# A graph network in float32: a deeper ring in its degree pass, a later `result`, and loads moved between queues

## The reference

```
h   = relu(layernorm(x))
A   = relu((adj + adj.T) / 2);  D = rowsum(A);  s = D ** -0.5
x   = x + relu((I - s[:,None] * A * s[None,:]) @ (h @ W0))        # layer 0
h   = relu(layernorm(x))
x   = x + diag(adj) @ h @ W1[0] + triu(adj,1) @ h @ W1[1] + tril(adj,-1) @ h @ W1[2] + bias   # layer 1
```

## Time and profile before

| what | value |
|---|---|
| median of 3 runs | 955.57 us (954.47 to 959.18) |
| profiled execution | 955.61 us |
| its span | 953.9 us |
| PE busy | 912.2 us, 96% |
| DVE, ACT, POOL busy | 554.6, 487.0, 289.6 us |
| moved by DMA | 212.69 MB, mean 223 GB/s |
| granted clock of PE, mean | 0.995 |

### The profile page before, as it was taken

One profiled execution on the slowest core, in us unless ns is written; L12 is line 12 of the kernel. 1 busy time (PEld: TensorE's weight loads), 2 busy tenths in 40 slices (PEclk: granted clock), 3 DMA queues, 4 the chain that ended last, 5 costly groups with the idle time before them and its releaser, 6 DMA issues.

```text
span 953.9 us, 17244 instructions
## 1 busy us (share of the span) xinstructions
PE 912.2 (96%) x4471; PEld 768.4 (81%) x4471; DVE 554.6 (58%) x1475; ACT 487.0 (51%) x1026; POOL 289.6 (30%) x300
## 2 busy tenths in 40 slices
PE   3679999999999999999999999899999999999998
PEld 2558778888888888888888888688888888888886
DVE  4899677778787766565656565333333443344432
ACT  3797567676766765545554554233333333333331
POOL 4895344434434444443344332011111100000000
PEclk9999999999999999999999999899999999999999
DMA  9995899999999985556555653766666655555552
GB/s 285 328 282 146 282 326 328 341 325 346 336 328 335 323 316 179 159 178 196 164 158 176 195 192 113 237 185 191 190 182 188 190 167 164 168 162 159 163 169 68
DMA packets 179578, 212.69 MB, mean 223 GB/s; under 512 B 13648, under 2 KB 114000, under 8 KB 177488
## 3 DMA queue, kind: packets, MB, share of 16 engines
q1 hardware_dynamic: 136816, 158.18, 54.4%
q10 hardware_dynamic: 42720, 54.01, 15.9%
HBM read 143.99 MB, written 68.16 MB: 222 GB/s over the span
## 4 chain that ended last, share of the span: by engine, by line
PE 84%; DVE 4%; DMA 4%; issue 3%; POOL 2%; SPq 2%; ACT 1%; ACTq 0%; DVEq 0%; POOLq 0%
PE psAcc L579 23%; PE psAcc L577 23%; PE psAcc L578 23%; PE psG L548 2%; PE psG L550 2%; PE psA L453 2%; PE psG L549 2%; PE psZ L489 2%; DMA colb<-in_adj 2%; DMA xp<-in_x 2%; PE psW L425 1%; POOL AT L1099 1%; PE psAcc L591 1%; PE psAcc L589 1%; PE psAcc L590 1%
## 5 line engine op out<-in xcount | busy, mean ns | idle before, releaser
L645 ACT ACTIVATE Lh<-C 128x512 fp32r<-128x512 f32 x256 | 161.3, 630 | 300.5 <-PE psAcc L579 250.1
L577 PE MATMUL psAcc<-Xh,Lh 128*128 128x512 f32 x496 | 200.2, 404 | 4.1 <-DVE Ll L838 4.0
L577 PE MATMUL psAcc<-Yh,Lh 128*128 128x512 f32 x512 | 200.9, 392 | 0.0
L579 PE MATMUL psAcc<-Yh,Ll 128*128 128x512 f32 x512 | 200.1, 391 | 0.0
L578 PE MATMUL psAcc<-Yl,Lh 128*128 128x512 f32 x512 | 199.9, 390 | 0.0
L579 PE MATMUL psAcc<-Xh,Ll 128*128 128x512 f32 x496 | 195.0, 393 | 0.0
L578 PE MATMUL psAcc<-Xl,Lh 128*128 128x512 f32 x496 | 194.4, 392 | 0.0
L838 DVE TENSOR_TENSOR Ll<-C,Lh 128x512 fp32r<-128x512 f32 x128 | 90.8, 711 | 148.8 <-ACT Lh L645 148.8
L579 PEld LDWEIGHTS psAcc<-Yh,Ll 128*128 128x128 f32 x512 | 96.1, 188 | 20.3
L578 PEld LDWEIGHTS psAcc<-Yl,Lh 128*128 128x128 f32 x512 | 96.2, 188 | 19.0
L577 PEld LDWEIGHTS psAcc<-Xh,Lh 128*128 128x128 f32 x496 | 93.8, 189 | 21.6 <-issue 4.9
(11 more groups left out here) (134 smaller groups left out, 1348.0 us busy)
## 6 DMA issues: line engine op xcount, KB each, us to landing
C<-at_dram SPq DMA_DIRECT2D x128, 256.0 KB, 2.7
at_dram<-AT SPq DMA_DIRECT2D x16, 1088.0 KB, 5.4
s_dram<-C ACTq DMA_DIRECT2D x64, 256.0 KB, 5.3
R<-in_adj SPq DMA_DIRECT2D x64, 256.0 KB, 5.8
g_dram<-g ACTq DMA_DIRECT2D x32, 512.0 KB, 3.3
C<-s_dram SPq DMA_DIRECT2D x64, 256.0 KB, 3.9
C<-in_adj SPq DMA_DIRECT2D x60, 256.0 KB, 5.3
t_dram<-x ACTq DMA_DIRECT2D x32, 256.0 KB, 2.2
```

The costliest lines, as they stand in the source:

```text
L577: mm(acc, lh, rh[:, k, :], start=k == 0, stop=False)
L579: mm(acc, ll, rh[:, k, :], start=False, stop=c < L1 and k == NB - 1).then_inc(used, 1)
L645: A(Lh[:, q, :], C[:, q, :], ACT.Relu if s.c < L1 else ACT.Copy).then_inc(lhi, 1)
```

## The change

It does five things. The ring `sring` holds six chunks instead of four, so that DVE's sum n waits for ACT's and POOL's work on chunk n-6; there are four sets of statistics instead of three; yTs becomes a seventh turn buffer. The loads of the weights and of the first two tiles of x go from SP's queue to the head of ACT's, and PE waits for the weights only before the first product with W0. `load_next` no longer loads R for step 2: SP issues these four loads at the end of the prologue, each after PE's transposes of step 1's R. The load of the next xp is split off `turned_xp` as `load_xp`, and in step 1 it is called earlier in ACT's body. `result` of step 34 moves to where that of step 33 is: ahead of `split_lo(nxt, 2)`.

```diff
+RING = 6
...
-            sring = sb("sring", [P, 4, 4 * P], at=early)
+            sring = sb("sring", [P, RING, 4 * P], at=early)
...
-            n0s = [Norm(f"n{u}", early, 2 * HB) for u in range(3)]
+            n0s = [Norm(f"n{u}", early, 2 * HB) for u in range(4)]
...
-        T0 = [z[:, :], h2[:, :], g12[:, 0, :], g12[:, 1, :], x1[:, 1, :], xe[:, :]]
+        T0 = [z[:, :], h2[:, :], g12[:, 0, :], g12[:, 1, :], x1[:, 1, :], xe[:, :], yTs[:, :]]
...
         def _(sp):
-            sp.dma_start(W0[:, :], w_l0).then_inc(ld_w, 16)
-            sp.dma_start(x1[:, 0, 0:3 * F].rearrange("p (k o) -> p k o", k=3),
-                         w_l1.rearrange("k f o -> f k o")).then_inc(ld_w, 16)
...
-                    if g < TILES_WITH[0]:
-                        load_tiles([g])
...
-                if 2 <= s.c <= NB:
+                if 3 <= s.c <= NB:
                     load_rows(s, q)
...
             for q in range(1, NQ - 1):
                 load_next(Step(None, 1), q)
+            for q in range(NQ):
+                sp.wait_ge(rT, q + 1)
+                load_rows(Step(None, 2), q)
...
             def times_W0(j):
 
+                if j == 0:
+                    pe.wait_ge(ld_w, 32)
...
-            pe.wait_ge(ld_w, 32)
             def chunk_T(n):
...
             A = nc.scalar.activation
+            for j in range(TILES_WITH[0]):
+                act.dma_start(blocks(hst[:, node(j), :]), xv[0, node(j)]).then_inc(ld_x0[j], 16)
+                if j == 0:
+                    act.dma_start(W0[:, :], w_l0).then_inc(ld_w, 16)
+                    act.dma_start(x1[:, 0, 0:3 * F].rearrange("p (k o) -> p k o", k=3),
+                                  w_l1.rearrange("k f o -> f k o")).then_inc(ld_w, 16)
             act.wait_ge(ld_w, 32)
...
             def turned_xp(t):
 
+                if t.c != 1:
+                    load_xp(t)
+                wait(act, yw_ok, t.of(1, 0))
+                A(yTs[:, :], psZ[:, :], ACT.Copy).then_inc(yT_ok, 1)
+
+            def load_xp(t):
+
                 wait(act, yT, t.of(1, 1))
-                wait(act, yw_ok, t.of(1, 0))
                 if t.c < NB - 1:
                     act.dma_start(blocks(xp[:, :]), xv[1, bass.ds(t.of(1, 1), 1)]
                                   .rearrange("o p b f -> (o p) b f")).then_inc(ld_xp, 16)
-                A(yTs[:, :], psZ[:, :], ACT.Copy).then_inc(yT_ok, 1)
...
                     A(hTh[:, :], psZ[:, :], ACT.Copy).then_inc(hThi, 1)
+                if c == 1:
+                    load_xp(t)
                 if 2 <= c < NB:
                     normal_xp(t)
...
-                    normal_done(dve, j - 4)
+                    normal_done(dve, j - 6)
...
-                if n >= 4:
-                    dve.wait_ge(p0R, n - 3)
-                    wait(dve, p0C, ADDS0[n - 3] + 1)
-                    wait(dve, cap, sum(1 for m in range(n - 3) if CH0[m][1] == 0))
+                if n >= RING:
+                    dve.wait_ge(p0R, n - RING + 1)
+                    wait(dve, p0C, ADDS0[n - RING + 1] + 1)
+                    wait(dve, cap, sum(1 for m in range(n - RING + 1) if CH0[m][1] == 0))
...
-                if c > L1 and c != L1 + 1:
+                if c > L1 + 2:
                     result(t)
...
-                if c == L1 + 1:
+                if L1 + 1 <= c <= L1 + 2:
                     result(t)
                 if c < LAST - 1:
                     split_lo(nxt, 2)
```

More of the change, by code:

```diff
@@ L605, in normal0 @@
                 act.wait_ge(s0_nm, j // 2 + 1)
-                n0, o = n0s[j // 2 % 3], HB * (j % 2)
+                n0, o = n0s[j // 2 % 4], HB * (j % 2)
                 for b in range(HB):
@@ L653, in rectify @@
                 act.wait_ge(p0S, n + 1)
-                A(sring[:, n % 4, 0:w], sring[:, n % 4, 0:w], ACT.Relu, accum_out=drow[:, k, g:g + 1]).then_inc(p0R, 1)
+                A(sring[:, n % RING, 0:w], sring[:, n % RING, 0:w], ACT.Relu, accum_out=drow[:, k, g:g + 1]).then_inc(p0R, 1)
             def normal_xp(t):
@@ L871, in mean0 @@
                 dve.wait_ge(s0_rs, u + 1)
-                neg_mean(n0s[u % 3], s0_nm)
+                neg_mean(n0s[u % 4], s0_nm)
             def degrees(e):
@@ L902, in chunk_sum @@
                 dve.wait_ge(p0T, n + 1)
-                if n >= 4:
-                    dve.wait_ge(p0R, n - 3)
-                    wait(dve, p0C, ADDS0[n - 3] + 1)
-                    wait(dve, cap, sum(1 for m in range(n - 3) if CH0[m][1] == 0))
-                V.tensor_tensor(sring[:, n % 4, 0:w], psA[:, n % 2, 0:w],
+                if n >= RING:
+                    dve.wait_ge(p0R, n - RING + 1)
+                    wait(dve, p0C, ADDS0[n - RING + 1] + 1)
+                    wait(dve, cap, sum(1 for m in range(n - RING + 1) if CH0[m][1] == 0))
+                V.tensor_tensor(sring[:, n % RING, 0:w], psA[:, n % 2, 0:w],
                                 rowb[:, (NB - 1 - k) % 3, 4 * g * P:4 * g * P + w], ALU.add).then_inc(p0S, 1)
@@ L1093, in _ @@
                         pool.wait_ge(p0R, n + 1)
-                        G.tensor_copy(C[:, NQ - 1 - k // 4, (k % 4) * P:(k % 4 + 1) * P], sring[:, n % 4, 0:P]).then_inc(cap, 1)
+                        G.tensor_copy(C[:, NQ - 1 - k // 4, (k % 4) * P:(k % 4 + 1) * P], sring[:, n % RING, 0:P]).then_inc(cap, 1)
                     if BELOW0[n]:
@@ L1099, in _ @@
                         G.tensor_tensor(out=colacc[:, 4 * g * P:4 * g * P + w], in0=colacc[:, 4 * g * P:4 * g * P + w],
-                                        in1=sring[:, n % 4, 0:w], op=ALU.add).then_inc(p0C, 1)
+                                        in1=sring[:, n % RING, 0:w], op=ALU.add).then_inc(p0C, 1)
                         added[g] = ADDS0[n + 1] + 1
@@ L1107, in _ @@
                         pool.wait_ge(s0_ve, u + 1)
-                        power(n0s[u % 3].rs[:, :], n0s[u % 3].ve[:, :], mhalf[:, 0:2 * HB]).then_inc(s0_rs, 1)
+                        power(n0s[u % 4].rs[:, :], n0s[u % 4].ve[:, :], mhalf[:, 0:2 * HB]).then_inc(s0_rs, 1)
                 if XP_POWER == n:
```

## The result

| kernel | median | runs | lowest to highest | profiled execution, span |
|---|---|---|---|---|
| before | 955.41 us | 17 | 952.82 to 961.87 | 955.61, 953.9 |
| changed | 953.32 us | 17 | 951.00 to 955.08 | 951.12, 949.4 |

The ratio is 0.9971, with a 95% interval of 0.9957 to 0.9984: about 2.8 us less (1.5 to 4.1); the two medians alone are 2.1 apart. That is a gain, but a small one: less than half of the 6.0 us forecast, within 0.5% of no change, and at the upper end of the range. The two profiled executions alone show 4.5 us. Two later measurements of the changed kernel gave 0.9985 and 0.9972.

The account below looks back on a forecast made before the run. The prediction took DMA stream, then DVE, to bound the degree pass and PE every step from about 97 us. Its terms, 4.4 + 1.3 + 0 + 0.3 = 6.0 us, took 955.6 to 949.6 us, range 945.5 to 953.5.

Parts of the forecast that it names:

- The late result: Step 34: moving `result` later on DVE ends PE's 4.0 us wait at L577 and the half speed behind; gain 4.4 us.
- the slow part costs 2.5: After the L577 wait in step 34: 15 matmuls at half clock took 5.97 us instead of 3.45.
- (a): Rival: after the 2.0 us wait before step 35 PE runs at half speed, costing 2.5 us, total 952.1; chance 0.2.
- Cover of 0.6 us, so I cost this at nothing: Step 35: loads behind SP's late store still let DVE finish by 618, before PE needs the last quarter at 618.6.
- The first loads: Kernel's beginning: SP issues fewer loads ahead of its first row block, so the stream starts earlier; gain 1.3 us.
- the stretch before full rate is what can shrink: First 5 us, DMA at only 104 GB/s: this shrinks by 0.9 to 2.0 us, taken as 1.3.
- It reaches the end of the pass: Degree pass: the 1.3 us won at the start lasts to its end, as stream and DVE follow each other until 90 us.
- Ring, sets, turn buffers: Degree pass: the deeper ring, extra statistics set and turn buffer gain 0, since DVE's chunk sums waited for PE only.
- Rows of step 2, early xp: Steps 1 and 2: PE's 1.25 us wait for R goes, mostly into the wait at L489; gain 0.3 us.
- (b): Rival: the beginning gives nothing, as weights land late on ACT and latency already held the stream; total 950.9, chance 0.1.
- (c): Rival: the beginning gives more, as the ring removes DVE idling and PE's early waits shrink; total 946.3, chance 0.15.
- (d): Rival: loads behind SP's late store move the stall to steps 35 and 36, 6.5 us each; total 960.5, chance 0.05.

Follow-up runs that it names:

- e1: The kernel before with only `result` of step 34 moved late: 954.20 us, ratio 0.9984 to the kernel before.
- e2: The changed kernel with `result` of step 34 put back early: 955.90 us, ratio 1.0004 to the kernel before.
- e3: The changed kernel with the weight loads and first two tiles of x back in SP's queue: 953.57 us, ratio 0.9984 to the kernel before.
- e4: The changed kernel with no edit, measured again: 954.10 us, ratio 0.9985 to the kernel before.
- e6: The changed kernel with PE's turn of the first xp two blocks earlier in step 0: 952.62 us, ratio 0.9970 to the kernel before.
- e10: The changed kernel with ACT's two weight loads ahead of its loads of x tiles: 952.14 us, ratio 0.9966 to the kernel before.
- e11: The changed kernel with ring of four, three statistics sets and six turn buffers again: 953.65 us, ratio 0.9988 to the kernel before.
- e12: The changed kernel with no edit, a third profile: 952.51 us, ratio 0.9972 to the kernel before.
- e7: The kernel before with no edit, for a second profile: 955.06 us.
- e8: The kernel before with no edit, for a third profile: 954.17 us.
- e5: The changed kernel with step 33's x1 reload issued earlier and step 34's `result` and copy behind its first low half: 951.65 us, ratio 0.9955 to the kernel before.
- e9: The changed kernel with weights and first x tiles back on SP, earlier x1 reload, `result` and copy, earlier first xp turn: 951.03 us, ratio 0.9948 to the kernel before.

## Why the prediction was only partly right

**The late result: right mechanism, term mis-sized.** The wait at L577 went, and a wait for L1051's copy came at the start of step 35, of 1.44 us where 2.0 was foreseen. e1 and e2 show that the gain is the late result's.

Between the two profiled executions the stretch of the table above went from 30.51 to 26.16, by 4.35, and the forecast said 4.4. That agreement was luck: one execution stood for each end. The four kernels with the early result have a mean of 29.7, the eight with the late one (changed, e1, e3, e4, e6, e10, e11, e12) a mean of 27.1: 2.7 us.

The step that failed is "the slow part costs 2.5": it took the 6.8 us of half speed of one execution as the price of the stall, but the other three that have the stall, e2, e7 and e8, ran slow for 3.4 us. That is 0.8 of the 1.7 by which 4.4 was too large. The other end is less smooth too: the wait before step 35 was between 1.4 and 2.8 over the runs, 1.9 in the mean, as foreseen; but rival (a), half speed behind it, came in two of eight (e3, e6), 0.4 in the mean.

The second step that failed is "Cover of 0.6 us, so I cost this at nothing". It followed the last quarter and the reload, which did hold, but not the copy at the end of DVE's step, which PE's step 36 waits for: PE moved 5.35 us forward and the loads behind the late store 0.6, and PE stood 0.45 to 1.1 us in the changed kernel, e1, e4, e10, e11 and e12, 0.5 in the mean of the eight.

The 2.7 is read from traces; the times alone have 1.4 (e1) and 1.8 (e2 against e4), each with an interval wide enough to hold it. e5, in which `result` and copy of step 34 come early in DVE's step because their reload does, has the stretch at 25.6, and e9 at 24.7, so the wait left before step 35 was avoidable.

**The first loads: no gain, and the degree pass ends about 1 us later.** The step that failed is "the stretch before full rate is what can shrink", costed at 1.3. SP issued earlier and nothing landed earlier. The columns of the second row tile, in the timeline of SP and the table of DMA issues up to 12 us (KB, median us to landing), first in the kernel before:

```profile
8.74 0.43 SPq L286 DMA_DIRECT2D colb<-in_adj  x1
...
colb<-in_adj SPq DMA_DIRECT2D x1, 896.0 KB, 10.1
```

and in the changed kernel:

```profile
7.12 1.10 SPq L282 DMA_DIRECT2D colb<-in_adj  x1
...
colb<-in_adj SPq DMA_DIRECT2D x1, 896.0 KB, 12.4
```

Issued 1.6 us earlier, they are there 0.7 later. In the first 5 us the DMA moved 96 GB/s, not more than 104. The rule of the Trainium skill weighed against this term (DMA: Bandwidth & Descriptors, Issuing engines are not separate DMA queues) was nearer, for it allows no gain but the issue time; by it the term was 0.9, and this too did not come.

"It comes 1 to 4 us later" was off as well: ACT's split came 5.8 us later. The kernel before has the first line of these, the changed kernel the second (same table):

```profile
x<-in_L_gnn_W SPq DMA_DIRECT2D x1, 192.0 KB, 2.6
```

```profile
x<-in_L_gnn_W ACTq DMA_DIRECT2D x1, 192.0 KB, 7.7
```

Ahead of everything on SP the weights landed in 2.6 us; behind a tile of x and beside SP's stream of adj they took 7.7. DVE's low part L842 (L855 of the changed kernel), which stands ahead of the first sum in DVE's queue, waited 9.2 us for ACT's split. That made the first sum late, by 2.1 us in the mean, but what the prediction set against it, DVE's idle time before the second row tile, did cover most of it. The means of the five traces with the old head (before, e1, e3, e7, e8) and the six with the new one (changed, e2, e4, e5, e11, e12), for some of DVE's chunk sums (starts, us) and the first turn of xp:

```
            1st sum   5th    13th   21st   28th   turn of xp
old head    8.5       20.2   34.8   48.1   61.0   97.0
new head    10.6      20.6   35.1   48.1   61.9   98.0
```

By the 21st sum nothing is left of the late start, so "It reaches the end of the pass" failed too: here a shift of the first sums did not. The 0.9 us that the turn of xp has later arise between the 21st and the 28th; from there to the turn all eleven take 35.9 to 36.4. So that the late weights cost this 1 us is not shown, and why the stretch from 48 to 62 us is longer with the new head stays open. What goes with it is PE's granted clock from 50 to 60 us. The stages of e8, e12 and e5, in this order:

```profile
50.00:60.00 10.00, 7.57 (x52) 5.81 (x50) 9.32 (x37) 10.00 (x29) 10.00 (x11) 1.00 1.11 320
```

```profile
50.00:60.00 10.00, 8.37 (x49) 7.46 (x50) 7.83 (x33) 8.13 (x24) 9.02 (x10) 0.83 1.10 307
```

```profile
50.00:60.00 10.00, 8.74 (x48) 7.96 (x49) 8.17 (x32) 7.50 (x22) 8.30 (x10) 0.72 1.09 309
```

Their turns of xp are at 96.3, 98.2 and 98.6. Over the eleven, 1.00 goes with 96.3 to 97.1, 0.83 to 0.87 with 97.1 to 98.3, 0.70 to 0.72 with 98.0 and 98.6, and at a like clock the new head is still 0.6 to 1.0 later. Which of clock and lateness brings the other was not tried. The size is rough, and the times of e3 and e4 don't confirm it. e6 and e9 have an edited turn, e10 a third head, so they aren't counted.

**Ring, sets, turn buffers: right, 0.** e11 has them at the old size, and the turn of xp moves by 0.02. Among the engines DVE's sums wait for PE alone in either.

**Rows of step 2, early xp: right, 0.25 for the 0.3.** Between the two profiled executions it looks like 0: the wait for R went and the wait at L489 took its whole 1.3. But other traces with the old place of these loads have more to lose. e7 and e8 wait for R also behind the turn of xp, as in this line of e7's timeline of PE, and half speed follows (a granted clock of 0.66 from 110 to 115 us):

```profile
110.45 1.06 PE L453 MATMUL psA<-ident,R 128*128 128x128 f32 x4 [0.81 <-DMA R<-in_adj]
```

In e1 the load of xp, which ACT issues at 113.93 there and at 109.69 in the changed kernel, lands late and holds DVE's statistics for 0.40: the early `load_xp`, costed at nothing, has a part in it. From the first turn of xp to the third the four traces with the old order (before, e1, e7, e8) take 28.87 to 29.26 us, the eight with the new order and the old turn 28.85 to 28.91: 0.25 less in the mean. The loads of step 1's last quarter stayed covered. e6 confirms that the chain starts at PE's turn.

**The rivals.** (a) happened, in two of eight for the 0.2 given, but it was worth 1.7 us (3.4 at half rate), not 2.5. (b) is what the beginning came to and a bit more. (c) finds no support: with the old ring (e11) the pass ends at the same time. (d) did not come: its mechanism, the reload behind the late store, is there, but at 0.45 to 1.1 us and not 6.5. Sum by what the traces have: 2.7 - 1.0 + 0 + 0.25 = 1.95 us, beside the 2.8 (1.5 to 4.1) of the runs.

## What to carry to other kernels

Before a stall is priced, look at it in several profiled executions: here the wait itself repeats within half a us (3.7 to 4.2), but the stretch of half speed behind it may be 3.4 or 6.8 us long, or absent. Moving an instruction to the end of an engine's step also moves the issue of every load behind it; here more was won by issuing earlier the load that the instruction waits for, together with its move forward (25.6 us for 27.1, e5). And a small load that an early instruction needs goes ahead of the large stream: on another engine's queue beside it the weights took 7.7 us for 2.6. Last, an early delay is followed to the end of its stage before it is priced: of 2.1 us at the first chunk sum nothing was left at the 21st.

## What the hardware showed that was not expected

Half speed followed some waits and not others of the same length. Before step 35 it came behind 1.98 us (e3) and 2.0 (e6), but not behind 2.35 (e4) or 2.81 (e11). At L489 in step 2 it came behind 2.08 (e1), 2.21 (e5), 2.22 (e6) and 2.23 (e9), but not behind 2.19 (e4), 2.20 (e12), 2.21 (e11) or 2.24 (e10). From that turn to the last product of step 33 the first four took 471.2 to 471.5 us and the other ten traces 469.5 to 470.0, which gives its price as about 1.6 us. Why one wait brings it and another of its length does not was not settled: nothing was tried that changes PE's work ahead of a wait while the wait stays the same.
